# Second-layer projection weights scaled and turned during the local attention, first keys and queries split by VectorE in pieces, two projection pairs placed among the maxima

## The reference

```python
x = x + attention_layer(layernorm(x))      # first layer; the window attention is its last part
# second layer, on h0 = layernorm(x)
h = rmsnorm(h0, ln1_w)
qkv = h @ wqkv.T                           # 16 query heads, 4 key and 4 value heads of 16 columns
q, k = rope(q), rope(k)                    # rotation by cos and sin tables
scores = q @ k.T * 0.25, causal
attn = softmax(scores) @ v
x2 = h0 + attn @ wo.T
logits = rmsnorm(x2, ln2_w) @ gate_w.T     # router: the best 2 of 8 experts
out = x + x2 + sum(expert_e(h2) * weight_e)
```

## Time and profile before

| | |
|---|---|
| median of 3 runs | 1780.33 us (1775.42 to 1781.79) |
| the profiled execution | 1763.21 us, of which the span of the trace is 1761.1 us |
| busy share of the span | PE 93%, DVE 66%, ACT 54%, POOL 32% |
| stage4 | from 161.7 to 270.5 us of the span |
| stage6, preparations and first maxima | 271.8 to 368.6 us |
| stage6, steady loop | 368.6 us to about 1216 us |
| mean granted clock of PE | 0.962 of full speed |

### The profile page before, as it was taken

The page is one execution under the profiler, slowest core; times in us unless marked ns, Lnnn a source line. Parts: engine busy times, 40 slices in busy tenths (PEclk is TensorE's granted clock), DMA queues, the critical chain, the costliest instruction groups (busy, mean ns, idle before and its releaser), DMA issues. The chain is left out here.

```text
span 1761.1 us, 29631 instructions
## 1 busy us (share of the span) xinstructions
PE 1642.4 (93%) x9072; PEld 814.3 (46%) x9072; DVE 1154.3 (66%) x3177; ACT 947.0 (54%) x2065; POOL 557.6 (32%) x847
## 2 busy tenths in 40 slices
PE   7998996899999999999999999998896699999996
PEld 3476654433333333333333333332785355555554
DVE  6502686699888888888888888881585234343342
ACT  6223552346767667676776767677574233333332
POOL 2124235554513203012030210000277244444443
PEclk9999997879999999999999999999996899999999
DMA  5000001303030020301103021000378477777774
GB/s 162 1 1 1 1 1 25 60 2 62 2 61 2 15 48 2 61 2 31 32 2 61 2 40 23 2 1 1 94 236 285 101 131 130 129 131 129 131 126 71
DMA packets 252098, 105.50 MB, mean 60 GB/s; under 512 B 208032, under 2 KB 247848, under 8 KB 251944
## 3 DMA queue, kind: packets, MB, share of 16 engines
q1 hardware_dynamic: 233296, 80.62, 21.4%
q0 software_dynamic: 13296, 18.23, 6.1%
q10 hardware_dynamic: 5352, 4.76, 0.8%
HBM read 30.61 MB, written 23.67 MB: 31 GB/s over the span
## 5 line engine op out<-in xcount | busy, mean ns | idle before, releaser
L1590 ACT ACTIVATE prob<-pS 128x512 f32<-128x512 f32 (+3 forms) x1280 | 597.7, 534 | 256.2 <-PE pS L1465 134.1
L1668 DVE TENSOR_REDUCE mx<-pM 128x1 f32<-128x512 f32 x768 | 502.9, 685 | 70.9 <-PE pM L1445 67.2
L1445 PE MATMUL pM<-KT,QT 96*128 96x512 bf16 (+3 forms) x1280 | 444.3, 358 | 10.4 <-DMA QT<-Qt 7.7
L1461 PE MATMUL pS<-QT,KT 99*128 99x512 bf16 (+3 forms) x1280 | 416.2, 350 | 3.9 <-ACT prob L1590 2.8
L1480 PE MATMUL pO<-prob,VV 128*32 128x512 f32 (+3 forms) x2560 | 299.9, 540 | 14.6 <-ACT prob L1590 14.3
L2348 PE MATMUL pH<-w13T,QKV 128*128 x568 | 256.6, 595 | 22.3 <-ACT QKV L2374 22.3
L1664 DVE CUSTOM_DVE_ANT_0 junk<-pM,mask_row 128x128 bf16<-128x128 f32 (+3 forms) x512 | 241.3, 483 | 51.4 <-PE pM L1445 48.0
L1445 PEld LDWEIGHTS pM<-KT,QT 96*128 96x128 bf16 x1280 | 124.2, 98 | 270.8 <-DVE mx L1668 110.0
L1368 POOL CAST mpart<-mneg 128x16 bf16<-128x16 f32 x32 | 6.8, 213 | 655.7 <-DVE mneg L1676 655.7
L2407 DVE TENSOR_TENSOR QKV<-QKV,pH 128x512 f32<-128x512 f32 x71 | 48.8, 687 | 240.0 <-issue 203.5
L1461 PEld LDWEIGHTS pS<-QT,KT 99*128 99x128 bf16 x1280 | 123.4, 98 | 143.2 <-ACT prob L1590 79.6
(11 more groups left out here) (342 smaller groups left out, 1955.2 us busy)
## 6 DMA issues: line engine op xcount, KB each, us to landing
raw<-in_ffn_w_dram SPq DMA_DIRECT2D x48, 256.0 KB, 3.8
QKV<-queue SPq DMA_DIRECT2D x71, 136.0 KB, 2.5
out_dram<-x ACTq DMA_DIRECT2D x8, 512.0 KB, 4.6
x<-_attn_hidden_states_dram SPq DMA_DIRECT2D x14, 256.0 KB, 5.5
QKV<-QKV SPq DMA_TRANSPOSE x142, 3.2
QT<-mrow SPq DMA_DIRECT2D x128, 3.0 KB
out_dram<-QKV POOLq DMA_INDIRECT x71, 3.8
wc_s<-in_attn_Wc_dram SPq DMA_DIRECT2D x1, 1024.0 KB, 8.3
```

The lines of the kernel that those rows point to most:

```text
L1445: last = nc.tensor.matmul(pM[:, bank, 0:w], QT[0:ROWS, par, h, qt * P:(qt + 1) * P], KT[0:ROWS, par, 512 * part:512 * part + w], start=Tru ...
L1461: last = nc.tensor.matmul(pS[:, p % NSC, lo:512], KT[0:ROWS + 3, par, kt * P:(kt + 1) * P], QT[0:ROWS + 3, par, h, 512 * c + lo:512 * c + ...
L1590: nc.scalar.activation(prob[:, n % 3, h, lo:512], pS[:, p % NSC, lo:512], ACT.Exp, scale=SCALE).then_inc(s.head_exp, 1)
L1668: nc.vector.reduce_max(mx[:, h, qt, part:part + 1], pM[:, plan.bank[item], 0:w], AX.X).then_inc(s.unit_max, 1)
```

## The change

Four things are changed.

1. The loads of ln1_w, wqkv, wo and gate_w, the scaling, and the turning of the blocks move from the start of `stage6` into `stage4`. SP issues the loads at the start of `stage4`. DVE does the products ahead of the first tile's maximum and the subtractions behind it. PE turns one block of 128 rows per tile in the tiles t = 21 to 26 (two transposes each, behind `tile_transposes`), and ACT copies it out with one instruction in place of DVE's two. `wqkvT`, `woT` and `gwT` now live from the start of the kernel on.
2. Rotations of the first batch: POOL takes the tiles 1, 3, 5, 7, 9, 11, 13, and DVE the other nine. DVE's `moments` are spread behind other rotations.
3. DVE splits the first group's keys, and then its queries in two halves of two heads. SP's first transposes wait for keys, first half and second half apart (`first_ready` 1, 2 and 3). POOL no longer has a `prepare(0)`.
4. P14 stands behind the third unit of the maxima on PE and ACT, and P15 behind the seventh.

For room, `stage7`'s small tiles (junk, tri, lg, pr, hot, picked, both) now lie in `wqkvT`'s place; its instructions and their order stay as they are.

```diff
@@ stage4
+        FIRST = len(pieces) - 3
+            @block.sync
+            def _(sp):
+                sp.dma_start(ln1_b[:, :], v.ln1_w.partition_broadcast(P)).then_inc(s.ln_in, 16)
+                sp.dma_start(raw[:, 0:3, :], v.wqkv.rearrange("(t p) h -> p t h", p=P)).then_inc(s.raw_in, 16)
+                sp.dma_start(raw[:, 3:5, :], v.wo.rearrange("(t p) h -> p t h", p=P)).then_inc(s.raw_in, 16)
+                sp.dma_start(raw[0:E, 5, :], v.gate_w).then_inc(s.raw_in, 16)
...
+                def turn_weight(n):
+                    rows = weight_rows(n)
+                    if n == 0:
+                        pe.wait_ge(s.w_ready, 3)
+                    if n < 2:
+                        pe.wait_ge(s.qk_out, len(pieces))
+                    else:
+                        pe.wait_ge(s.wT_out, n - 1)
+                    src = scaled[:, n, :] if n < 3 else raw[0:rows, n, :]
+                    for c in range(C):
+                        last = nc.tensor.transpose(pQK[:, n % 2, c * P:c * P + rows], src[:, c * P:(c + 1) * P],
+                                                   ident[0:rows, 0:rows])
+                    last.then_inc(s.wT_mm, 1)
...
                     tile_transposes(t)
+                    if FIRST <= t < FIRST + 6:
+                        turn_weight(t - FIRST)
...
+                def weight_out(n):
+                    act.wait_ge(s.wT_mm, n + 1)
...
+                    if FIRST <= t < FIRST + 6:
+                        weight_out(t - FIRST)
                     if t + 1 < T:
                         values(t + 1)
...
+                dve.wait_ge(s.ln_in, 16)
+                dve.wait_ge(s.raw_in, 48)
+                for n in range(3):
+                    nc.vector.tensor_tensor_reduce(scaled[:, n, :], raw[:, n, :], ln1_b[:, :], 1.0, 0.0, ALU.mult, ALU.add,
+                                                   wsum[:, 0, n:n + 1]).then_inc(s.w_times, 1)
                 most(0)
+                dve.wait_ge(s.w_times, 3)
+                nc.vector.tensor_scalar(wsum[:, 1, :], wsum[:, 0, :], 1.0 / H, None, ALU.mult).then_inc(s.w_mean, 1)
...
@@ Plan
+PAIRS_AHEAD = 6
-        self.front = [("P", i) for i in range(NP // 2, NP)] + units
+        pairs = [("P", i) for i in range(NP // 2, NP)]
+        self.front = pairs[:PAIRS_AHEAD] + [x for n, unit in enumerate(units)
+                                            for x in (pairs[PAIRS_AHEAD + n // 4:PAIRS_AHEAD + n // 4 + 1] if n % 4 == 3 else []) + [unit]]
@@ stage6
+        ON_POOL = (1, 3, 5, 7, 9, 11, 13)
+        ON_DVE = tuple(t for t in range(TB) if t not in ON_POOL)
...
+                    else:
+                        sp.wait_ge(s.tile_pad, 3)
+                        sp.wait_ge(f.first_ready, 1)
                     sp.dma_start_transpose(KT[:, gi % 2, :].rearrange("p (t n) -> p t n", n=P),
...
                     for h in range(GRP):
+                        if gi == 0:
+                            sp.wait_ge(f.first_ready, 2 + h // 2)
...
-                prepare(0)
                 values_in(0)
...
-                pe.wait_ge(f.raw_in, 48)
-                for n in range(6):
...
-                pe.wait_ge(f.wT_out, 12)
                 for i in range(NP // 2):
                     projected_pair(i)
...
+                for n in range(NDVE):
+                    rotate(dve, nc.vector, ON_DVE[n], n, byc_dve, bys_dve, f.by_dve, f.turned_dve)
+                    if n in (0, 2, 4, 5, 6, 7):
+                        moments((0, 2, 4, 5, 6, 7).index(n) + 2)
+                dve.wait_ge(f.turned_dve, NDVE)
+                dve.wait_ge(f.turned_pool, NPOOL)
                 first = Chain(dve, s.first_chain)
-                split_queries(nc.vector, first, s.first_copied, 0, 0, [rem[:, r] for r in range(2)])
+                split(nc.vector, first, s.first_copied, QKV[:, 0:TB, NH * HD:(NH + 1) * HD],
+                      lambda n: Kt[:, :, n * HD:(n + 1) * HD], PARTS_K, [rem[:, r, :, 0:HD] for r in range(2)])
                 dve.wait_ge(s.first_copied, 3)
-                assert first.k == 5
...
+                dve.sem_inc(f.first_ready, 1)
+                for half in range(2):
+                    split_queries(nc.vector, first, s.first_copied, 0, 0, 2 * half, 2 * half + 2, [rem[:, r] for r in range(2)])
+                    dve.wait_ge(s.first_copied, 6 + 3 * half)
+                    dve.sem_inc(f.first_ready, 1)
```

More of the change, by code:

```diff
@@ L1008, in stages_layer2 @@
         ln2_b = sb("ln2_b", [P, H], F32, late)
-        woT = sb("woT", [P, C, H], F32, late)
-        gwT = sb("gwT", [P, C, E], F32, late)
+        woT, gwT = v.woT, v.gwT
         pad_at = sb("pad_at", [P, E], I32, late)
@@ L1318, in _ @@
                 pool.wait_ge(f.small_in, 48)
-                for n in range(TB // 2):
-                    turn(2 * n + 1)
-                    if n % 2 == 0:
+                for n in range(NPOOL):
+                    turn(ON_POOL[n])
+                    if n % 2 == 0 and n < 8:
                         root(n // 2 + 2)
@@ L1492, in _ @@
                 turn(0)
-                pe.wait_ge(f.raw_in, 48)
-                for n in range(6):
-                    rows = E if n == 5 else P
-                    if n < 3:
-                        pe.wait_ge(f.w_ready, n + 1)
-                    src = scaled[:, n, :] if n < 3 else raw[0:rows, n, :]
-                    for c in range(C):
-                        k = 2 * n + c
-                        if k >= 2:
-                            pe.wait_ge(f.wT_out, k - 1)
-                        nc.tensor.transpose(pM[:, k % 2, 0:rows], src[:, c * P:(c + 1) * P],
-                                            ident[0:rows, 0:rows]).then_inc(f.wT_mm, 1)
-                pe.wait_ge(f.wT_out, 12)
                 for i in range(NP // 2):
@@ L1619, in _ @@
-                dve.wait_ge(f.w_mean, 1)
-                for n in range(3):
-                    nc.vector.tensor_scalar(scaled[:, n, :], scaled[:, n, :], wsum[:, 1, n:n + 1], None,
-                                            ALU.subtract).then_inc(f.w_ready, 1)
-                k = 0
-                for n in range(6):
-                    for c in range(C):
-                        dve.wait_ge(f.wT_mm, k + 1)
-                        rows = E if n == 5 else P
-                        dst = (wqkvT[:, c, n * P:(n + 1) * P] if n < 3 else v.woT[:, c, (n - 3) * P:(n - 2) * P]
-                               if n < 5 else v.gwT[:, c, :])
-                        nc.vector.tensor_copy(dst, pM[:, k % 2, 0:rows]).then_inc(f.wT_out, 1)
-                        k += 1
@@ L1632, in _ @@
                 moments(1)
                 dve.wait_ge(f.small_in, 48)
-                for n in range(TB // 2):
-                    rotate(dve, nc.vector, 2 * n, n, byc_dve, bys_dve, f.by_dve, f.turned_dve)
-                    if n % 2 == 0:
-                        moments(n // 2 + 2)
-                moments(6)
-                moments(7)
-                dve.wait_ge(f.turned_dve, TB // 2)
-                dve.wait_ge(f.turned_pool, TB // 2)
+                for n in range(NDVE):
+                    rotate(dve, nc.vector, ON_DVE[n], n, byc_dve, bys_dve, f.by_dve, f.turned_dve)
+                    if n in (0, 2, 4, 5, 6, 7):
+                        moments((0, 2, 4, 5, 6, 7).index(n) + 2)
@@ L1648, in _ @@
-                dve.wait_ge(s.qchain, 5)
-                dve.wait_ge(s.kparts, 3)
-                dve.sem_inc(s.qchain, 5)
-                dve.sem_inc(s.kparts, 3)
+                dve.sem_inc(f.first_ready, 1)
[3 more added lines that the diff above has]
+                    dve.sem_inc(f.first_ready, 1)
+                assert first.k == 15
```

108 lines of the change are left out of this document (56 added, 52 removed).

## The result

| | median | runs | ratio to before, 95% interval |
|---|---|---|---|
| before | 1778.80 us | 1775.42 to 1781.79 (6) | |
| after | 1767.12 us | 1761.55 to 1767.97 (6) | 0.9924 [0.991, 0.9937] |

The ratio is worth 0.0076 × 1778.8 = 13.5 us, and the medians differ by 11.7 us; 14.8 was predicted. The profiled execution took 1767.04 us, with a span of 1765.3 us. That span is 4.2 us longer than the profiled one of before, though the median is 11.7 us shorter, so the spans alone can't be compared; where in the span the time comes and goes can.

What follows compares the result with a forecast made beforehand. PE bounds the steady loop (busy 393 of 400 us), so only its start, set by stage6's chain over several engines, could move: 15.3 − 0.5 for stage4 = 14.8 us; 1780.3 − 14.8 = 1765.5 us, range 1758 to 1774.

Steps and rivals of the forecast that it cites:

- Weights out of stage6: Start of stage6: rms, not PE, is ACT's last wait; DVE's first rotation 9.9 us earlier, full clock at about 279.
- Rival 4: The slower outcome, chance 0.04; where in the kernel and its size are not in the text given.
- stage4 for 0.5: In stage4: the moved weights work was charged 0.5 us in all, against the gain.
- the 0.2 charged for the tiles: In stage4's tiles 21 to 26: transposes and ACT's copy fit into waits; 0.2 us charged, 4.5 if neither fitted.
- the 0.3 for the start: At stage4's start: DVE's subtractions ahead of the second maximum cost 0 to 1.2 us, taken as 0.3.
- Rival 2: In stage4: six tiles at 0.75 and 1.2 us at its start cost 5.7 us; 1770.7 us, chance 0.08.
- Seven and nine: stage6's rotations, seven on POOL, nine on DVE: DVE ends last at 309.7, 11.9 us earlier than the former 321.61.
- rival 1: stage6's preparations: DVE becomes the long pole; ninth rotation +1.8, keys +3.4, first half +0.7; 1771 us, chance 0.13.
- Splits: DVE's splits in stage6: 2.4 us for the keys, 3.5 for each half of the queries.
- The place of P14 and P15: First chunk's maxima: placing the pairs among units worth nearly nothing, end at 332.6 against 332.9 with them ahead.
- Rival 3: Steady loop: its start moves but its end does not, the time is given back; 1778 to 1781 us, chance 0.08.
- the clock as 0: PE's clock up to the loop's start: warm start could give 1 us, cold stretch take 1; taken as 0.

Runs made afterwards that it cites:

- after_again: The changed kernel run again unedited, for a second trace; 1762.98 us, ratio to before 0.9933.
- placing_only: The kernel before with only wqkvT, woT and gwT kept for the whole kernel and stage7's small tiles in wqkvT; 1775.32 us, ratio 0.9999.
- no_weights: The changed kernel with the weights made in stage6 as before, all else of the change kept; 1774.80 us, ratio to before 0.998.
- eight8: The changed kernel with POOL's eighth rotation given back, so eight rotations on each engine; 1767.07 us, ratio to before 0.9929.
- roots_early: The changed kernel with POOL's root(0) ahead of its masks and pads, and DVE writing Kt's and Qt's pads; 1764.26 us, ratio to before 0.9915.
- whole_q: The changed kernel with DVE splitting the queries in one piece instead of two halves; 1769.64 us, ratio to before 0.9943.
- roots_pairs8: The changed kernel with the edits of roots_early and pairs8 together; 1759.52 us, ratio to before 0.9904.
- pairs8: The changed kernel with P14 and P15 ahead of all units of the maxima (PAIRS_AHEAD = 8); 1760.26 us, ratio to before 0.991.
- pairs_late: The changed kernel with P14 and P15 in the second chunk's maxima, ahead of units 22 and 34; 1763.14 us, ratio to before 0.9915.

## Why the prediction was right

1765.5 us was predicted and 1767.12 measured, a gain of 14.8 and one of 13.5 us by the ratio (11.9 in after_again, 11.7 by the medians of before and after). The mechanism was right. That the first trace met the sum to 0.1 us was partly luck: terms that were too cheap and too dear cancelled, and the trace was a quick one. By its steps:

- **Weights out of stage6: right.** First rotation predicted at 7.4, measured 7.42; ACT waits 3.23 us for rms, and PE's granted clock, 0.50 in the stretch from 276, is 0.89 in the one from 280 and 1.00 in the one from 284, with PE busy for 4.00 of 4 us in each; P0's products took 5.15 us and P1's 2.75. Rival 4, the slower outcome, at 0.04, didn't come: the ratio is 0.9924.
- **stage4 for 0.5: the charge was not there; that the sum fits is luck.** 31 of the 32 maxima of its loop come 1.44 to 1.46 us later, the eighth 1.15. Of this 0.99 is there before stage4's first instruction (162.74 for 161.75), ahead of any instruction of the change. Its cause is open: that start lies between 161.3 and 161.8 in the three traces of before and between 161.7 and 162.7 in the other eleven, 162.46 in placing_only. The other 0.46 arises between there and the first maximum (12.19 us for 11.73), but the kernels with the weights in stage4 have 11.58 to 12.44 there, placing_only, which has none, 12.16, and no_weights 12.43. So it is no cost of the weights either: the difference is in PE's first projection products, which stand in every kernel. Timeline of after, first maximum and then one tile with a block of weights:

```profile
174.92 0.23 DVE L988 TENSOR_REDUCE nmax<-pS 128x1 f32<-128x64 f32 x1 [1.11 <-PE pS L856]
...
242.57 0.22 DVE L988 TENSOR_REDUCE nmax<-pS 128x1 f32<-128x64 f32 x1
...
242.82 0.31 ACT L950 ACTIVATE block_p<-pS,nmax 64x64 f32<-64x64 f32 x1 [1.07 <-DVE nmax L988]
...
243.10 0.30 PEld L880 LDWEIGHTS pO<-V,probT 97*128 97x128 f32 x2 [0.27 <-DVE probT L1000]
```

  The three products fit into DVE's wait, which shrinks from the 2.26 of the earlier trace rows to 1.11. In the tile at 242.57 the block costs PE a part of its wait (0.27 left of the 0.49 in the earlier trace rows) and no time: 242.57 − 174.92 is the 241.12 − 173.47 of before to the hundredth. From the first maximum to the last it takes 88.2 to 88.3 us in all 14 traces. Neither the 0.2 charged for the tiles nor the 0.3 for the start was there. Rival 2 is out.
- **Seven and nine: right in the first trace, a little short in the others.** The ninth rotation was predicted to end at 309.7 − 271.9 = 37.8. It ended at 37.10 there and at 39.1 to 39.4 in four others, so DVE with POOL beside it needs 1.3 to 1.6 us more than the term. This is most of the first of rival 1's three costs (1.8). In after_again the last rotation itself ran at 0.46, 0.48, 0.33 and 0.32 us with POOL through with its rotations, and the splits took 3.20 us for the keys and 4.11 for the first half of the queries. The loss is in the rotations before, next to POOL's: DVE's fifth to seventh took 2.78, 2.96 and 3.09 us in after_again, and 1.50, 1.98 and 2.00 in the first trace. But POOL had something to do, against what the prediction said: it computed `rms`, at 309.99 for 1.01 us, and by the records DVE's product at 310.50 ran inside that instruction and took 0.46 us. In all 14 traces, such products with nothing but `rms` of POOL beside them took 0.45 to 0.49 us; beside POOL's rotations they took 0.45 to 1.18, and every one above 0.49 had a rotation's instruction of POOL (160 or 320 columns) beside it.
- **Splits: 1.4 us too cheap together.** Keys 313.52 − 310.50 = 3.02 us, not 2.4, and a half 317.77 − 313.52 = 4.25, not 3.5: near rival 1's 4.2. The first landing (322.32 − 317.77 = 4.55 against 5.0) and the earlier rotations made up for it in the first trace, where the first unit is at 48.95 for a predicted 48.7.
- **The place of P14 and P15, "worth nearly nothing": the step that failed.** The first trace comes out at 60.64 for 60.7, but the comparison behind it was wrong. From the first unit to the first `mneg` it takes 11.7 us with the pairs between when PE has stood 1.88 us, and 12.65 (within 0.01) in each of after_again, eight8, roots_early and no_weights, where it has stood for 3.2 to 4.5 us and P14's products take 3.99 to 4.44 us in place of 2.75; in whole_q, where it has stood 6.43 us, it is 13.5. With the pairs ahead, the first unit came right behind P15, at 52.5 and 52.7 in the two traces, and 7.18 us follow where no head is late (roots_pairs8; 9.0 in pairs8, with its late third head): 59.8. Between, the end is the first landing plus 11.7 or 12.65, so it ties only with a landing at 48.1 or 47.2; it was at 48.95 in the first trace and at 50.1 to 51.5 in after_again, eight8, roots_early and pairs_late. I had compared the two at a single landing time and took the clock as 0. What it leaves out is that one order hands on every delay of DVE and the queue, and the other covers it. It costs the kernel 2.1 us by the traces of pairs8 and after_again and 3.1 by those of roots_pairs8 and roots_early. The timed ratios point the same way (0.991 against 0.9924 and 0.9933, 0.9904 against 0.9915), but their intervals overlap, so the size rests on single traces.
- **Rival 3, the end doesn't move: out by the timed runs.** The loop's gain and the gain by the ratio stand within 1.9 us of each other in eleven of the twelve rows; pairs_late is 3.9 off, inside its interval.

From the first trace's loop's gain of 15.4 to the 12.3 of after_again it is 2.2 us for the rotations (39.30 − 37.10) and 0.95 for P14 (12.65 − 11.7).

## What to carry to other kernels

Take the work that only happens to be first out of a chain, and put it where an engine already waits in each turn of a loop: six blocks of weights cost stage4's tiles nothing and brought 10 of the 12 to 13.5 us. An item placed among waiting ones is not filler when the wait ahead of it is a transfer that moves with every delay upstream: price both orders at the early and at the late end of that landing, with the clock as it is after the wait, and prefer the one whose end moves less. And where several engines share a stretch, profile the same code twice before a microsecond of one trace is explained.

## What the hardware showed that I had not expected

- PE's clock after a short stand: full after 1.88 us (products 2.75 us, granted 1.00 throughout), lower after 3.24 (4.44 us, granted 0.58 in the stretch from 336), 4.15 (4.27 us, granted 0.57 in the stretch from 324) and 6.43 us (4.64 us, granted 0.50 in the stretch from 328).
- The rotations of DVE and POOL side by side end differently from execution to execution of the same instructions: DVE 37.10 with POOL 36.65, or DVE 39.30 with POOL 35.39. One engine's loss is in part the other's gain. DVE's products were stretched, to 1.18 us at most, only beside POOL's instructions of 160 or 320 columns; beside its `rms` of 4 columns alone they took 0.45 to 0.49 us.
- A head's transpose holds SP's queue for 2.4 us by the earlier trace rows. The four heads together took 9.47 us of it in eight8 and 10.84 in pairs8, the shortest and the longest of the 14 traces, and pairs8's PE waited 2.87 us for the third head. The cause is open.
- The router's stage, whose transfers moved 304 GB/s in the stretch of before and 251 in that of after, varied by 18 us between traces (185.36 to 203.63), more than the whole effect of the change. Medians of timed runs are what tells there, not a pair of traces.
